# Second attention of a two-layer decoder: projection by pairs of batches inside the rounds, a new order of copies and divisions

## The reference

```python
scores = jnp.einsum('bhtd,bhsd->bhts', q, k) / math.sqrt(HD)
scores = scores + mask[None, None, :, :]
attn = jax.nn.softmax(scores, axis=-1)
y = jnp.einsum('bhts,bhsd->bhtd', attn, v)
y = y.transpose(0, 2, 1, 3).reshape(B, T, D)
return y @ wo.T
# then, outside:
x = _layernorm(x + _L1_attn_ref(x, ...), axis=-1)
x = _layernorm(x + _L1_xattn_ref(x, L1_xattn_k, fside_S2_0, ctx_2048, ctx_2048, 8), axis=-1)
```

## Time and profile before

| what | value |
|---|---|
| median of 3 runs | 847.89 us (845.76 to 848.6) |
| the profiled execution's own time | 848.14 us |
| its span, first to last instruction | 846.3 us |
| PE, DVE, ACT, POOL busy in the span | 782.1, 538.5, 359.8, 373.7 us |
| mean granted clock of TensorE | 0.969 |
| second attention, first scores to last division | 537.0 to 642.2 us |

### The profile page before, as it was taken

The page is one execution under the profiler, slowest core; times in us unless marked ns, Lnnn a source line. Parts: engine busy times, 40 slices in busy tenths (PEclk is TensorE's granted clock), DMA queues, the critical chain, the costliest instruction groups (busy, mean ns, idle before and its releaser), DMA issues. The chain is left out here.

```text
span 846.3 us, 12715 instructions
## 1 busy us (share of the span) xinstructions
PE 782.1 (92%) x4092; PEld 599.9 (71%) x4092; DVE 538.5 (64%) x1049; ACT 359.8 (43%) x843; POOL 373.7 (44%) x339
## 2 busy tenths in 40 slices
PE   7899999999969889999999997988887896999997
PEld 5788888888844457888888885754445343788886
DVE  4666666677678964333333357799984698864535
ACT  3555555555541062232323234368884001543422
POOL 2221212123118924656565643799972885521100
PEclk9999999999989979999999999999999897999999
DMA  9210101010201014433333340000000012000001
GB/s 317 65 51 25 50 25 50 25 50 27 68 13 43 20 58 112 131 112 107 112 107 116 90 121 10 1 2 1 2 2 1 25 50 69 0 16 17 1 1 50
DMA packets 27054, 45.24 MB, mean 53 GB/s; under 512 B 3424, under 2 KB 16608, under 8 KB 26752
## 3 DMA queue, kind: packets, MB, share of 16 engines
q1 hardware_dynamic: 27008, 44.65, 17.7%
HBM read 43.45 MB, written 1.18 MB: 53 GB/s over the span
## 5 line engine op out<-in xcount | busy, mean ns | idle before, releaser
L1479 PE MATMUL bank<-xTh,ringh 128*128 128x512 f32 x420 | 169.5, 403 | 0.6 <-DVE xTl L1150 0.6
L1480 PE MATMUL bank<-xTl,ringh 128*128 128x512 f32 x420 | 166.2, 396 | 0.0
L1481 PE MATMUL bank<-xTh,ringl 128*128 128x512 f32 x420 | 166.0, 395 | 0.0
L1219 DVE TENSOR_TENSOR arena<-bank,arena 128x512 f32<-128x512 f32 x48 | 33.2, 691 | 114.9 <-ACT arena L881 105.7
L1481 PEld LDWEIGHTS bank<-xTh,ringl 128*128 128x128 f32 x420 | 79.3, 189 | 18.9
L1479 PEld LDWEIGHTS bank<-xTh,ringh 128*128 128x128 f32 x420 | 79.6, 190 | 16.7 <-issue 1.6
L1480 PEld LDWEIGHTS bank<-xTl,ringh 128*128 128x128 f32 x420 | 79.5, 189 | 15.1
L632 POOL TENSOR_TENSOR arena<-arena 128x512 f32<-128x512 f32 x48 | 62.6, 1303 | 51.6 <-DVE HTl L1223 49.5
L881 ACT ACTIVATE arena<-bank 128x512 f32<-128x512 f32 x48 | 28.7, 598 | 126.1 <-PE bank L1481 126.0
L555 POOL CAST ringh<-ring 128x768 fp32r<-128x768 f32 x15 | 12.7, 846 | 152.4 <-DMA ring<-w_attn 149.4
L1517 PE MATMUL bank<-outh,HTh 128*128 128x256 f32 x192 | 54.9, 286 | 3.1 <-DVE outl L1064 1.2
(11 more groups left out here) (269 smaller groups left out, 1971.7 us busy)
## 6 DMA issues: line engine op xcount, KB each, us to landing
ring<-w_moe SPq DMA_DIRECT2D x24, 256.0 KB, 2.9
arena<-route SPq DMA_DIRECT2D x16, 384.0 KB, 4.1
ring<-w_attn SPq DMA_DIRECT2D x15, 384.0 KB, 3.2
toep<-toep SPq DMA_DIRECT2D x32, 128.0 KB, 2.1
arena<-route SPq DMA_DIRECT2D x16, 256.0 KB, 4.1
outring<-w_down SPq DMA_DIRECT2D x24, 128.0 KB, 2.1
outring<-wo_attn SPq DMA_DIRECT2D x16, 128.0 KB, 2.0
arena<-route SPq DMA_DIRECT2D x16, 128.0 KB, 4.0
```

The costliest lines, as they stand in the source:

```text
L1219: dve.tensor_tensor(H1[:, i % LAG, :], bank[:, 1 + i % 2, :], SG[:, i % 2, :], ALU.mult).then_inc(gu_done, 1)
L1479: pe.matmul(o, ringh[:, slot, wc], xTh[:, k, halves[j]], start=(k == 0), stop=False)
L1480: pe.matmul(o, ringh[:, slot, wc], xTl[:, k, halves[j]], start=False, stop=False)
L1481: ins = pe.matmul(o, ringl[:, slot, wc], xTh[:, k, halves[j]], start=False, stop=(k == DK - 1))
```

## The change

The output projection no longer waits for all eight batches. Batches are taken by pairs q: `turn_pair` transposes both batches of a pair into bank 5 (pair 3: bank 6), ACT's `evac_pair` copies them to two buffers `yT[q % 2]`, `project_out(b)` multiplies one batch into bank 5 (pair 3: bank 7), and DVE's `add_pair` adds x. Pair 0 is turned in round 8 and projected in rounds 9 and 10, added at the end of round 11; pair 1 is turned in round 12, projected in 13 and 14, added at the end of round 15. Pairs 2 and 3 come in the drain.

Values and turned values share bank 4 in the rounds, so that bank 5 is free. PE's `weigh(n-3)` moves to the end of round n and waits for the division before it; ACT's `evac_y(n-3)` stands at t = 4n+1; `norm_y(n-4)` on DVE stands between the second and the third mask. `PT` has twelve buffers instead of eight. In the drain `turn_y` uses banks 0 to 2, which the scores have left, and value 14 bank 3. Statistics and root of batches 0 to 3 are taken before the last divisions. POOL's bias products wait for the last turned tile only.

The diff, cut:

```diff
@@ -108,6 +108,16 @@
+def value_bank(n):
+    return 3 if n == 2 * B - 2 else 4
+def turned_bank(n):
+    return 4 if n < 2 * B - 4 else (n - 2 * B + 4) % 3
@@ -283,7 +293,9 @@
         yN = rN
-        yT = TC[:, 0, :, :, :]
+        spare = arena[:, ARENA - 4 * TOK:ARENA].rearrange("p (s n) -> p s n", s=8)
+        PT += [spare[:, i, :] for i in range(4)]
+        yT = [spare[:, i, :].rearrange("p (k b t) -> p k b t", k=DK, b=2) for i in (4, 5)]
@@ -383,6 +395,7 @@
         wo_done = sem("wo_done")
+        wo_added = sem("wo_added")
         l1_psum = sem("l1_psum")
@@ -710,7 +723,7 @@
                     rotate(6 + t // 11)
-            pool.wait_ge(wo_done, 4)
+            pool.wait_ge(turned, B * NKV)
             pool.wait_ge(bias1_in, 16)
@@ -918,35 +931,52 @@
                 act.wait_ge(turned, t + 1)
-                if t >= 8:
-                    act.wait_ge(weighed, t // 4 - 1)
-                act.activation(PT[t % 8], bank[:, 6 + t % 2, :], ACT.Copy).then_inc(turned_out, 1)
+                if t == 8:
+                    act.wait_ge(qkv_psum, 16)
+                if t >= 12:
+                    act.wait_ge(weighed, t // 4 - 2)
+                act.activation(PT[t % 12], bank[:, 6 + t % 2, :], ACT.Copy).then_inc(turned_out, 1)
...
                     act.wait_ge(y_turned, n - 1)
-                act.activation(SF[:, n % 2, :], bank[:, 4, :], ACT.Copy).then_inc(y_evac, 1)
+                act.activation(SF[:, n % 2, :], bank[:, value_bank(n), :], ACT.Copy).then_inc(y_evac, 1)
+            def evac_pair(q):
+                act.wait_ge(y_psum, q + 1)
+                if q >= 2:
+                    act.wait_ge(wo_done, q - 1)
+                act.activation(yT[q % 2].rearrange("p k b t -> p (k b t)"), bank[:, 5 + q // 3, :], ACT.Copy).then_inc(yt_evac, 1)
             for t in range(B * NKV):
-                if t % 4 == 2 and t >= 10:
-                    evac_y((t - 10) // 4)
+                if t % 4 == 1 and t >= 13:
+                    evac_y((t - 13) // 4)
+                if t % 16 == 15 and t >= 31:
+                    evac_pair((t - 31) // 16)
                 if t >= 4:
...
             evac_pt(B * NKV - 3)
-            evac_y(2 * B - 2)
+            evac_y(2 * B - 3)
             evac_pt(B * NKV - 2)
             evac_pt(B * NKV - 1)
+            evac_y(2 * B - 2)
+            act.wait_ge(ln_var, 7)
+            act.activation(sd[:, 0:B // 2], mv[:, 0:B // 2, 1], ACT.Sqrt, bias=eps[:, 0:1]).then_inc(ln_sd, 1)
             evac_y(2 * B - 1)
+            evac_pair(3)
+            act.wait_ge(ln_scale, 4)
+            for b in range(B // 2):
+                act.activation(xN[:, b, :], rN[:, b, :], ACT.Identity, bias=shift[:, b:b + 1],
+                               scale=rstd[:, b:b + 1]).then_inc(ln_x0, 1)
+            act.wait_ge(ln_var, 8)
+            act.activation(sd[:, B // 2:B], mv[:, B // 2:B, 1], ACT.Sqrt, bias=eps[:, 0:1]).then_inc(ln_sd, 1)
             for n, (k, j) in enumerate(((0, 0), (1, 0), (0, 1), (1, 1))):
-                act.wait_ge(y_psum, n + 1)
-                act.activation(yT[:, k, 4 * j:4 * j + 4, :], bank[:, 2 * k + j, :].rearrange("p (b t) -> p b t", b=4),
-                               ACT.Copy).then_inc(yt_evac, 1)
-            norm_and_turn(3)
+                act.wait_ge(xt_psum, 12 + n + 1)
+                act.activation(xT[:, k, j * HALF:(j + 1) * HALF], bank[:, 2 * k + j, :], ACT.Copy).then_inc(xt_act, 1)
             norm_and_turn(4, high=True)
@@ -1272,7 +1302,9 @@
                 dve.wait_ge(y_turned, n + 1)
-                y = bank[:, 5, :].rearrange("p (q m c) -> p q m c", q=REP, c=32)
+                y = bank[:, turned_bank(n), :].rearrange("p (q m c) -> p q m c", q=REP, c=32)
+                if n > 2 * B - 4:
+                    dve.wait_ge(yn_done, n + 1)
                 dve.reciprocal(yr[:], y[:, :, :, HD]).then_inc(y_rec, 1)
@@ -1280,6 +1312,11 @@
+            def add_pair(q):
+                dve.wait_ge(wo_done, q + 1)
+                dve.tensor_tensor(rN[:, 2 * q:2 * q + 2, :], bank[:, 5 + 2 * (q // 3), :].rearrange("p (b d) -> p b d", b=2),
+                                  xN[:, 2 * q:2 * q + 2, :], ALU.add).then_inc(wo_added, 1)
@@ -1293,6 +1330,8 @@
                         .then_inc(masked1, 1)
+                    if n >= 4 and t % 4 == 1:
+                        norm_y(n - 4)
                 if n == 0:
@@ -1306,11 +1345,44 @@
                     rope(5 + n)
-                if n >= 4:
-                    norm_y(n - 4)
-            for n in range(2 * B - 4, 2 * B):
-                norm_y(n)
-            norm(3, wo_done, [1, 2, 3, 4])
+                if n in (11, 15):
+                    add_pair((n - 11) // 4)
+            def statistics_of(first, end):
+                for b in range(first, end):
+                    ins = dve.bn_stats(st[:, b, :], rN[:, b, :])
+                return ins
+            def aggregate(first, end):
+                for b in range(first, end):
+                    ins = dve.bn_aggr(mv[:, b, :], st[:, b, :])
+                ins.then_inc(ln_var, 1)
+            def inverse_root(first, end, at):
+                dve.wait_ge(ln_sd, at)
+                link(dve.reciprocal(rstd[:, first:end], sd[:, first:end]))
+            norm_y(2 * B - 4)
+            dve.wait_ge(wo_added, 2)
+            link(statistics_of(0, B // 2))
+            aggregate(0, B // 2)
+            norm_y(2 * B - 3)
+            add_pair(2)
+            norm_y(2 * B - 2)
+            norm_y(2 * B - 1)
+            inverse_root(0, B // 2, 7)
+            dve.wait_ge(ln_x0, 12)
+            dve.scalar_tensor_tensor(shift[:], mv[:, 0:B // 2, 0], -1.0, rstd[:, 0:B // 2], ALU.mult, ALU.mult).then_inc(ln_scale, 1)
+            dve.wait_ge(wo_added, 3)
+            statistics_of(B // 2, B - 2)
+            add_pair(3)
+            dve.wait_ge(wo_added, 4)
+            link(statistics_of(B - 2, B))
+            aggregate(B // 2, B)
+            inverse_root(B // 2, B, 8)
+            for b in range(B // 2, B):
+                dve.scalar_tensor_tensor(xN[:, b, :], rN[:, b, :], mv[:, b, 0:1], rstd[:, b:b + 1].broadcast_to([P, D]),
+                                         ALU.subtract, ALU.mult).then_inc(ln_x1, 1)
@@ -1773,54 +1845,87 @@
                 pe.wait_ge(turned_out, 4 * n + 4)
+                if n <= 2 * B - 4:
+                    pe.wait_ge(yn_done, n + 1)
+                elif n == 2 * B - 2:
+                    pe.wait_ge(masked1, B * NKV)
+                else:
+                    pe.wait_ge(y_evac, n - (n == 2 * B - 1))
                 if n == 0:
-                    pe.wait_ge(yn_done, 1)
                     pe.wait_ge(rope_done, 16)
-                if n >= 1:
-                    pe.wait_ge(y_evac, n)
                 for m in range(4):
                     g = (4 * n + m) * (HD + 1)
-                    ins = pe.matmul(bank[32 * m:32 * m + 32, 4, :], Vn[:, g:g + 32], PT[(4 * n + m) % 8],
+                    ins = pe.matmul(bank[32 * m:32 * m + 32, value_bank(n), :], Vn[:, g:g + 32], PT[(4 * n + m) % 12],
                                     start=True, stop=True)
...
                 pe.wait_ge(y_evac, n + 1)
-                if n >= 1:
-                    pe.wait_ge(yn_done, n + 1)
+                if n == 2 * B - 4:
+                    pe.wait_ge(masked1, B * NKV)
+                if n == 2 * B - 1:
+                    pe.wait_ge(yn_done, 2 * B - 2)
                 for q in range(REP):
-                    ins = pe.transpose(bank[:, 5, q * S:(q + 1) * S], SF[:, n % 2, q * S:(q + 1) * S], ident)
+                    ins = pe.transpose(bank[:, turned_bank(n), q * S:(q + 1) * S], SF[:, n % 2, q * S:(q + 1) * S], ident)
                 ins.then_inc(y_turned, 1)
-            for n in range(2 * B + 4):
-                if n < 2 * B:
-                    scores1(n)
+            def turn_pair(q):
+                pe.wait_ge(yn_done, 4 * q + 5)
+                if 1 <= q < 3:
+                    pe.wait_ge(wo_added, q)
+                for k in range(DK):
+                    for b in (2 * q, 2 * q + 1):
+                        at = (2 * k + b % 2) * S
+                        ins = pe.transpose(bank[:, 5 + q // 3, at:at + S], yN[:, b, k * P:(k + 1) * P], ident)
+                ins.then_inc(y_psum, 1)
+            def project_out(b):
+                q = b // 2
+                pe.wait_ge(yt_evac, q + 1)
+                for k in range(DK):
+                    ins = pe.matmul(bank[:, 5 + 2 * (q // 3), (b % 2) * D:(b % 2 + 1) * D], yT[q % 2][:, k, b % 2, :],
+                                    wq1[:, k, O_W:O_W + D], start=(k == 0), stop=(k == DK - 1))
+                if b % 2 == 1:
+                    ins.then_inc(wo_done, 1)
+            for n in range(2 * B):
+                scores1(n)
                 if n == 0:
...
                     project1(5)
-                if 3 <= n < 2 * B + 3:
-                    weigh(n - 3)
                 if n >= 4:
                     turn_y(n - 4)
```

(42 more changed lines are left out.)

## The result

The changed kernel takes 851.68 us (median of 7 runs, 849.62 to 852.0) against 847.89 (7 runs, 845.76 to 848.6): ratio 1.0044, 95% interval 1.003 to 1.0059. It is slower by about 3.8 us, clear of noise. Its profiled execution took 851.13 us with a span of 849.3.

The account below looks back on a forecast made before the run. It took the ring PE to ACT to PE as the bound: added work +5.5, the hold +2.2, drain -4.2, together +3.5 us, 851.6 for the profiled execution and 851.4 for the median; own range 849 to 855, 8-in-10 range 845.5 to 855.0.

Parts of the forecast that it names:

- Four projections on the bound: Rounds 9, 10, 13, 14: each added projection costs PE 0.90 us in full, 3.6 us together.
- Two groups of transposes 1.0 us and two copies in the ring 1.0 us: Rounds 8 and 12: PE's four transposes cost 0.48 us each round; their ACT copies, between copies PE awaits, 0.49 us.
- The sign given for rounds 8 and 12: In the new profile, score groups should stand about 6.4 us apart at rounds 8 and 12.
- the hold: Rounds 3 to 8 and 12: the late Exp of tile 4n delays the values' copy PE needs, 2.2 us in all.
- The two sums on DVE: End of rounds 11 and 15: two sums of 0.69 us cost 0, or 0.5 us if uncovered.
- forecast's second bound: Chain through late maximum, Exp, values' copy and PE: two rounds need 11.56 us instead of 11.00.
- The wait of probabilities 59 in the drain: In the drain, probabilities 59 wait for a copy behind the late Exp and a values' copy, costing 1.2 us.
- Rival 1: Rounds and drain: the Exp does not hold the values' copy, 3.4 us absent, 848.0 us, no change; chance 0.20.
- Shift: Drain's layer norm: DVE's tiny shift instruction, away from POOL's bias products, falls from 1.47 to 0.2 us, gaining 1.3.
- The drain, 29.8 us: From round 15's scores to POOL's first product for the convolution: 29.8 us instead of 33.97, 4.2 us shorter.
- rival 2: Six rounds: PE's gaps swallow 4.3 us of moved work, the hold at most half, giving 846.0 us; chance 0.17.
- rival 3: Drain: the clock falls inside it and PE's work slows, 3 to 5 us more, 855.5 us; chance 0.10.

Follow-up runs that it names:

- Experiment 3: Changed kernel with half of the output projection of batches 0 to 3 left out (one of two matmul groups each): 848.52 us, ratio to before 1.0019.
- experiment 2: Changed kernel with ACT's copy of a turned pair one tile later: 848.96 us, ratio to before 1.002.
- experiment 6: Changed kernel with values' copy ahead of the Exp, pair's copy later, and in the drain last weighing earlier, ACT's root behind last values' copy: 844.65 us.
- experiment 1: Changed kernel with ACT's values' copy of round n-3 ahead of the Exp of tile 4n instead of behind it: 848.07 us, ratio to before 1.0009.
- Experiment 5: Kernel before with only POOL's wait changed, so the bias products start at the last turn of probabilities: 845.7 us, ratio 0.9982.
- experiment 7: Kernel before's round order, twelve `PT` buffers, all four pairs in the drain on banks 0 to 3, bias products at the last turn: 842.79 us, ratio 0.9954.

## Why the prediction was right

It gave 851.4 us, and 851.68 was measured. That the two are 0.3 us apart is in part luck, since the executions of one kernel spread over 2 to 3 us. The sum holds by its parts: +7.37 against +7.7 in the rounds, -4.04 against -4.2 in the drain, +3.33 against +3.5 together; the profiled executions differ by 3.0 us, the medians by 3.8. Point by point:

- *Four projections on the bound, 3.6 us.* Measured 0.87 in each of four rounds, 3.5. Experiment 3 took half away, and 87 to 96% of that half came off.
- *Two groups of transposes 1.0 us and two copies in the ring 1.0 us.* The copies' price was shown by experiment 2: 0.48 in each of two rounds. The transposes were not tried apart; with the mends of experiment 6 round 8 takes 5.94 us, 0.44 over 5.50, which fits them. The sign given for rounds 8 and 12, about 6.4 us, left out the hold that the sum has there; 6.89 and 6.90 were measured.
- *The two sums on DVE, 0.* Nearly. With the hold gone, round 12, behind the first of these sums, takes 0.20 us more than round 8 (6.63 and 6.43 in experiment 1, 6.14 and 5.94 in experiment 6). The rows of experiment 6 show the place: PE's turn of pair 1 waits for the sum and starts 0.18 us late. In the changed kernel the hold covers it (6.89 and 6.90). The prediction looked for this price on DVE; it lies in PE's wait for DVE.
- *The hold, 2.2 us.* Experiment 1 gave back 1.94 in the rounds. Rounds 8 and 12 had 0.46 and 0.27 of it, rounds 4 and 6 0.75 and 0.46. By pairs of rounds the forecast's second bound is seen more plainly: rounds 3 and 4 take 11.48 us, 5 and 6 11.47, and rounds 7 and 8 and rounds 11 and 12 12.40 each, that is 11.47 and 0.93 for transposes and copy. The bound was thus 11.47, not 11.56, and a turn costs 0.46 over two rounds of 5.50, not 0.56. Against the old rounds 3 and 4 (10.83 us) the first turn costs 0.65. Rounds 3 and 4 take 10.74 without the hold (experiment 1), which is why the first turn gave back 0.75.
- *The wait of probabilities 59 in the drain, 1.2 us to be gained without the hold.* Experiment 1's drain shortened by 0.24 us until the last projection. Rival 1's price of 3.4 us was thus 1.1 to 1.2 us too high. In experiment 1 ACT does not wait for POOL at this place; it waits 0.83 us for PE's weighing before it can copy the values (635.43), and the Exp and the copy of probabilities 57 stand behind that copy, so probabilities 59 still wait 1.23 us instead of 1.46.
- *Shift, 1.3 us.* Experiment 5: 1.30, in the kernel before; in the changed kernel the row fell to 0.16 us, and its own price there was not tried apart.
- *The drain, 29.8 us.* 29.92, with each wait at its forecast place: projections ended at 24.0 against 24.1, and POOL followed the last normalization (660.46) by 1.73 us, where I took 1.5: the clock fell at 660.2, among the last transposes. In experiment 2, where it was full through them, POOL followed by 1.59 us.
- Rival 1 (no hold) fell by the row of ACT and by experiment 1, rival 2 by experiment 3, rival 3 by the clock, full until 660.2.

What the prediction did not see is that its own last sentence on the drain pointed at the better kernel: if PE's waits there are uncovered, pairs belong there and not in rounds without free time.

## What to carry to other kernels

In an in-order pipeline, look for gaps of the bounding engine at the very place in its order where the moved work will stand; here the rounds had none but the waits between turns of probabilities, which the projections behind them could not fill. The kernel with two pairs in the rounds (experiment 6) spends 4.4 us more there, and the one with these pairs in the drain (experiment 7) only 1.4 us more in the drain; the two differ in their order besides, so these are prices of whole arrangements. When an instruction is moved, follow what it now stands behind on its own engine as well as what it makes late on the next: the late maximum was harmless alone and cost 2 us once the values' copy stood behind the Exp. A bottleneck over two rounds shows as an alternation (6.42, 5.50, 5.97, 5.51), and the length of two rounds together, not of the longest one, gives the price.

## What the runs showed of the hardware

The shift instruction on DVE (128 by 4 elements, two operands in SBUF) took 1.47 us beside a product on POOL that reads SBUF, ending with it, and 0.16 us without one, in the same kernel otherwise (experiment 5). Beside the second product the four statistics, with one operand in SBUF, took 1.39 us, and 1.40 us in the changed kernel without a product beside them. In the changed kernel the same products ran beside divisions, whose rows (0.26 and 0.29 us) are those of before, and beside a sum with one operand in PSUM, 0.69 us. The Trainium skill (SBUF — State Buffer, Who interferes with whom) says that a DVE instruction with two inputs in SBUF contends with a GpSimd instruction that reads SBUF, and one with at most one such input, outside the 2-port modes, does not; the rows named here agree with it.

TensorE's granted clock did not always fall inside a gap of its work. It fell inside a gap of 3.13 us in the kernel before (653.6); in experiment 5 it stayed full through a gap of 1.83 us and fell at 652.2, and in the changed kernel through one of 2.18 us and fell at 660.2, both times while PE was at work. No run here tests what decides it.
